# The rows of B in a Mamba scan: TensorE's selecting products and ScalarE's copies, or SBUF-to-SBUF DMAs

## The chip, the cores and the metric

The kernel runs on one core of one Trainium2 chip. The metric is device time in microseconds: the median of three runs is 295.14 us (293.34 to 295.16). The profile is one such execution; its span is 295.0 us.

## What is computed

A block of a model on x (4 batches of 256 tokens by 256 channels, float32) and a context of 4 x 256 x 128. A gated state-space layer runs on the context, and a quantised feed-forward layer behind it. Around the change stands the state-space layer:

```python
x = einsum('ed,bld->bel', in_proj_w, hidden_states)       # 256 channels, then a causal conv of 4 taps
u = silu(xc + conv_b[None, :, None])
x_dbl = einsum('ke,bel->bkl', x_proj_w, u)                # 8 + 16 + 16 rows of 256 tokens
dt_lo, Bm, Cm = x_dbl[:, :8], x_dbl[:, 8:24], x_dbl[:, 24:]
delta = softplus(einsum('er,brl->bel', dt_proj_w, dt_lo) + dt_proj_b[None, :, None])
A = -exp(A_log)                                           # 256 channels x 16 states
def step(state, xs):                                      # over the 256 tokens
    d_t, B_t, C_t, u_t = xs
    dA = exp(d_t[..., None] * A)
    state = state * dA + (d_t * u_t)[..., None] * B_t[:, None, :]
    y_t = einsum('ben,bn->be', state, C_t)
    return state, y_t
y = (y + D * u) * silu(z)
```

For each of the 16 states, row n of B (256 tokens, the same for all channels) multiplies delta * u of every channel. The channels lie on the 128 partitions (in two halves), so a row of B is needed on all 128 partitions.

## The kernel before

The work is cut into 32 steps: 4 batches of 8, each step with NB = 2 of the 16 states. The program is written out by hand for each engine, and each engine runs its list in order. Semaphores stand between the engines. A step m goes like this:

- **The rows of B.** `B_rows(m)` on TensorE: two products of a one-column selector (`sel`) with `bc3`, which holds B and C as three bf16 pieces, put the step's two rows on all 128 partitions in PSUM, in the half `PB` of the tensor `BC`. `copy_B(m)` on ScalarE copies them to `Bs[:, m % 4]` in SBUF. There is one `PB`, so product m waits for copy m - 1. `Bs` has RING = 4 places, so copy m waits until the drives of step m - 4 have read theirs.
- **The drives.** `drives(m)` on GpSimd multiplies du = delta * u by `Bs` (two instructions of 128x512). Steps 0 and 1 are done by VectorE (`first_drive`).
- **The decays.** `decays(m)` on ScalarE: four exponentials, behind the copy of the same step.
- **The scan** on VectorE, in its list in step order; it takes decay and drive, both kept in rings of four. GpSimd's drives m wait for scan m - 4.
- **The rows of C**, selected the same way by TensorE into `PC`, the product with them on VectorE (`times_C`), and TensorE's transposing sum of the products (`accumulate`).

B's rows, decays and drives are written AHEAD = 4 steps ahead of the scan. Between these steps stand, in the same lists, the front of batch k + 2 (projection, softplus), the norm and gate products of batch k - 1, and the quantised down projection of batch k - 2. What is left of batches 2 and 3 follows the last step. At the start, SP issues the loads of the inputs, four of them of 1 MB; afterwards SP has only the eight stores of the output (128 KB each), each after a wait for its result (L300 to L302). `high_pieces(n)` on ScalarE (L772) takes the first bf16 piece of batch n's B and C out of PSUM.

Of the kernel before, what the change touches and what calls it, by code (L numbers as in the profile page):

```python
# [12 lines left out]
P = 128  # L13
# [4 lines left out]
LC = L // P  # L18
# [36 lines left out]
def gated_ssm_ffn(nc, x, ctx_1024, g_xattn, g_ffn, in_proj_w, conv_w, conv_b, x_proj_w, dt_proj_w, dt_proj_b,  # L55
                  A_log, D, w_gate, w_up, w_down, ident, hadamard, out):
    stack = ExitStack()
    with stack:
        def sb(name, shape, dt=F32):
            return stack.enter_context(nc.sbuf_tensor(name, shape, dt))  # L60

        def sem(name):
            return stack.enter_context(nc.semaphore(name))
# [54 lines left out]
        diag = sb("diag", [P, HALF, P])  # L118

        Bs = sb("Bs", [P, RING, NB, L])  # L120
        decay = sb("decay", [P, RING, HALF, NB, L])
        drive = sb("drive", [P, RING, HALF, NB, L])
        state = sb("state", [P, STATES, HALF, NB, L])
# [64 lines left out]
        act_tap, dve_conv, dve_drive = sem("act_tap"), sem("dve_conv"), sem("dve_drive")  # L188
        had_built, dve_fold, pool_fold_last = sem("had_built"), sem("dve_fold"), sem("pool_fold_last")

        pe_B, act_B, act_decay, pool_drive, dve_scan, pe_C, dve_prod, pe_acc = (
            sem(n) for n in ("pe_B", "act_B", "act_decay", "pool_drive", "dve_scan", "pe_C", "dve_prod", "pe_acc"))

        pe_xin, dve_inwk, act_conv, act_u, pe_xdbl, dve_split, act_dtlo, pe_draw = (
            sem(n) for n in ("pe_xin", "dve_inwk", "act_conv", "act_u", "pe_xdbl", "dve_split", "act_dtlo", "pe_draw"))
# [9 lines left out]
            sem(n) for n in ("pool_fold", "pe_tp", "act_tp", "pe_h", "dve_sc", "act_tq", "dve_q2", "pe_q2T", "dve_q2T",  # L205
                             "pe_dn", "dve_out"))
        stored = [sem(f"stored_{t}") for t in range(LC)]

        pool_front_link = Chain(sem("pool_front_link"), 4)
        dve_front_link = Chain(sem("dve_front_link"), 3)  # L210
# [68 lines left out]
        @block.sync  # L279
        def _(sp):  # L280
            cr = tiles(ctx_1024)
            sp.dma_start(ctxs[:, 0], cr[:, 0:LC]).then_inc(ld_ctx0, 16)
            sp.dma_start(inw[:], in_proj_w.rearrange("(h p) d -> p h d", p=P)).then_inc(ld_inw, 16)
            sp.dma_start(xpw[:], x_proj_w).then_inc(ld_small, 16)
            sp.wait_ge(zeroed, 1)
            sp.dma_start(dtw[:, :, DT0:DT0 + DR], dt_proj_w.rearrange("(h p) r -> p h r", p=P)).then_inc(ld_small, 16)
            with nc.allow_non_contiguous_dma(reason="one value per partition"):
                for dst, src in ((cb, conv_b), (dtb, dt_proj_b), (dskip, D)):
                    sp.dma_start(dst[:], src.rearrange("(h p) -> p h", p=P)).then_inc(ld_conv, 16)
            sp.dma_start(ctxs[:, 1:B].rearrange("p b c d -> p (b c) d"), cr[:, LC:B * LC]).then_inc(ld_ctx, 16)  # L290
            sp.dma_start(wnat[:, 0].rearrange("p (a h) -> p a h", a=NI),
                         w_gate.rearrange("(a p) h -> p a h", p=P)).then_inc(ld_w[0], 16)
            sp.dma_start(xs[:].rearrange("p b c d -> p (b c) d"), tiles(x)).then_inc(ld_x, 16)
            sp.dma_start(wnat[:, 1].rearrange("p (a h) -> p a h", a=NI),
                         w_up.rearrange("(a p) h -> p a h", p=P)).then_inc(ld_w[1], 16)
            sp.dma_start(wnat[:, 2].rearrange("p (o i) -> p o i", o=HALF),
                         w_down.rearrange("(o p) i -> p o i", p=P)).then_inc(ld_w[2], 16)
            sp.dma_start(had[:], hadamard).then_inc(ld_had, 16)
            for b in range(B):
                for t in range(LC):  # L300
                    sp.wait_ge(dve_out, LC * b + t + 1)
                    sp.dma_start(tiles(out)[:, LC * b + t], ot[:, t]).then_inc(stored[t], 16)  # L302
            for t in range(LC):
                sp.wait_ge(stored[t], 16 * B)

# [2 lines left out]
        def _(pe):  # L308
# [36 lines left out]
            def setup_late():  # L345
# [4 lines left out]
                        at = (b - 1) * L + P * c  # L350
                        last = nc.tensor.transpose((PC if at < 512 else PY)[:, at % 512:at % 512 + P], ctxs[:, b, c], id32[:])
                last.then_inc(pe_setup, 1)

            def B_rows(m):

                b, j = divmod(m, STEPS)
                pe.wait_ge(dve_split, b + 1)
                pe.wait_ge(act_high0, b + 1)
                if m >= 1:
                    pe.wait_ge(act_B, m)  # L360
                else:
                    pe.wait_ge(act_setup, 2)
                for n in range(NB):
                    last = nc.tensor.matmul(PB[:, L * n:L * (n + 1)], row_pick(NB * j + n), bc3[:, b, :],  # L364
                                            start=True, stop=True)
                last.then_inc(pe_B, 1)

            def C_rows(m):
                b, j = divmod(m, STEPS)
# [11 lines left out]
            def row_pick(r):  # L381
                return sel[:, r:r + 1].to_broadcast([3 * 2 * DS, P])
# [140 lines left out]
            def hadamard_mm(f, t):  # L523

                pe.wait_ge(act_tp, LC * f + t + 1)
                if f == t == 0:
                    pe.wait_ge(had_built, 1)
                if (f, t) == (B - 2, 1):
                    pe.wait_ge(act_B, B * STEPS)
                    pe.wait_ge(dve_prod, B * STEPS)  # L530
                elif (f, t) == (B - 1, 0):
                    pe.wait_ge(act_tq, LC * f)
                elif f == B - 1:
                    pe.wait_ge(dve_mul, LC * f + 2)
                elif t == 0:
                    pe.wait_ge(dve_mul, LC * f + 2)
                else:
                    pe.wait_ge(act_tq, LC * f + 1)
                dst = transform_bank(f, t)
                for a in range(NI):  # L540
                    if f < B - 1:
                        last = nc.tensor.matmul(dst[:, E * (a // 2):E * (a // 2 + 1)], hT[:, t, a, :],  # L542
                                                had2[:, a % 2].rearrange("p i c -> p (i c)"),
                                                start=(a % 2 == 0), stop=(a % 2 == 1))
                    else:
                        last = nc.tensor.matmul(dst[:, P * a:P * (a + 1)], hT[:, t, a, :], had2[:, 0, 0],  # L546
                                                start=True, stop=True)
                last.then_inc(pe_h, 1)
# [53 lines left out]
            pe.wait_ge(dve_consts, 1)  # L602
            x_dbl(0)
            dt_proj(0)
            B_rows(0)
            setup_late()
            B_rows(1)
            in_proj(1, [0])
            B_rows(2)
            in_proj(1, [1])  # L610
            C_rows(0)
            for m in range(3, AHEAD):
                B_rows(m)
            for k in range(B):
                p, f, n = k - 2, k - 1, k + 2
                old, new, front = p >= 0, f >= 0, n < B
                for s in range(STEPS):
# [17 lines left out]
                    if s == 7:  # L635
                        if k == 0:
                            weight_T(5)
                    if g + AHEAD < B * STEPS:
                        B_rows(g + AHEAD)
                    if s == 1:  # L640
                        if k == 0:
                            x_dbl(1)
# [74 lines left out]
        def _(act):  # L717
# [4 lines left out]
                act.dma_start(gates[:, 1:2], g_ffn.partition_broadcast(P)).then_inc(ld_gate, 16)  # L722
                act.dma_start(alog[:], A_log.rearrange("(h p) n -> p h n", p=P)).then_inc(ld_gate, 16)

            def copy_B(m):
                act.wait_ge(pe_B, m + 1)
                if RING <= m < RING + DVE_DRIVES:
                    act.wait_ge(dve_drive, m - RING + 1)
                elif m >= RING:
                    act.wait_ge(pool_drive, drives_before(m - RING + 1))  # L730
                nc.scalar.copy(Bs[:, m % RING], PB.rearrange("p (n l) -> p n l", n=NB)).then_inc(act_B, 1)  # L731

            def decays(m):

                b, j = divmod(m, STEPS)
# [36 lines left out]
            def high_pieces(n):  # L772

                act.wait_ge(pe_xdbl, n + 1)
                if n >= 1:
                    act.wait_ge(dve_split, n)
                nc.scalar.copy(high[:], front_bank(n)[0:2 * 2 * DS, 0:L]).then_inc(act_high, 1)
                nc.scalar.copy(bc3[4 * DS:6 * DS, n], front_bank(n)[4 * DS:6 * DS, 0:L]).then_inc(act_high0, 1)
# [97 lines left out]
            act.wait_ge(pe_setup, 5)  # L876
            nc.scalar.copy(inwT[:].rearrange("p k e -> p (k e)"), UP[:]).then_inc(act_setup, 1)
            softplus(0)
            copy_B(0)
            act.wait_ge(pe_setup, 6)  # L880
            nc.scalar.copy(ctxT[:, 1:3], PC.rearrange("p (b l) -> p b l", b=2))
            nc.scalar.copy(ctxT[:, 3], PY[:, 0:L]).then_inc(act_setup, 1)
# [5 lines left out]
            act.wait_ge(decay_zeroed, 1)  # L888
            decays(0)
            for m in range(1, AHEAD):  # L890
                copy_B(m)
                decays(m)
            for k in range(B):
                p, f, n = k - 2, k - 1, k + 2
                old, new, front = p >= 0, f >= 0, n < B
                for s in range(STEPS):
# [19 lines left out]
                        if front:  # L916
                            high_pieces(n)
                    if g + AHEAD < B * STEPS:
                        copy_B(g + AHEAD)
                        decays(g + AHEAD)  # L920
                    if s == 0:
                        if k == 0:
# [52 lines left out]
        def _(pool):  # L975
            def drives(m):

                b, j = divmod(m, STEPS)
                pool.wait_ge(act_B, m + 1)
                pool.wait_ge(du_ready, b + 1)  # L980
                if m >= RING:
                    pool.wait_ge(dve_scan, m - RING + 1)
                for h in range(HALF):
                    last = nc.gpsimd.tensor_tensor(  # L984
                        drive[:, m % RING, h], du[:, b % 2, h, :].unsqueeze(1).to_broadcast([P, NB, L]),
                        Bs[:, m % RING], ALU.mult)
                last.then_inc(pool_drive, 1)
# [104 lines left out]
        def _(dve):  # L1092
# [48 lines left out]

            def first_drive(m):

                dve.wait_ge(act_B, m + 1)
                dve.wait_ge(du_ready, 1)
                for h in range(HALF):
                    last = nc.vector.tensor_tensor(drive[:, m, h], du[:, 0, h, :].unsqueeze(1).to_broadcast([P, NB, L]),
                                                   Bs[:, m], ALU.mult)
                last.then_inc(dve_drive, 1)
# [281 lines left out]
def tiles(t):  # L1431

    return t.rearrange("b l n -> (b l) n").rearrange("(c p) n -> p c n", p=P)
# [30 lines left out]
```

## Time and profile before

| | |
|---|---|
| median of 3 runs | 295.14 us (293.34 to 295.16) |
| span of the profiled execution | 295.0 us |
| VectorE busy | 255.7 us, 87% |
| GpSimd busy | 191.1 us, 65% |
| TensorE busy | 180.2 us, 61% |
| ScalarE busy | 163.9 us, 56% |
| first scan starts, last scan starts | 26.5 us, 241.2 us |
| bytes moved by DMA | 6.29 MB, nearly all in the first 22 us |

PE is TensorE's matmuls, PEld its weight loads, DVE VectorE, ACT ScalarE, POOL GpSimd, SPq the sequencer that issues DMAs. A name such as L984 is line 984 of the kernel before. Idle time is given with what ended it ("releaser"). Steps of the loop are not even: other work of VectorE lies between the scans.

### The profile page before, as it was taken

What the parts mean: (1) busy time and instruction counts of PE and PEld (TensorE: products, weight loads), DVE (VectorE), ACT (ScalarE), POOL (GpSimd) and SP (SyncE); (2) the same over time, 40 slices, a digit from 0 to 9 for tenths busy, and PEclk for the clock granted to TensorE, in tenths of its full rate; (3) what the DMA queues carried; (4) which work ended last, traced back from release to release, by engine and by line L of the source; (5) the groups of instructions that cost most, each with busy time, mean ns of one, the idle gap of its engine ahead of it and who ended that gap; (6) DMA issues with size and microseconds to landing.
All of it is one profiled execution on the core that took longest, in us unless ns stands there. A gap on an engine that the chain in (4) does not pass through costs nothing. (4 is left out here: it accounts for less than half of the span.)

```text
span 295.0 us, 3093 instructions
## 1 busy us (share of the span) xinstructions
PE 180.2 (61%) x988; PEld 140.0 (47%) x988; DVE 255.7 (87%) x295; ACT 163.9 (56%) x286; POOL 191.1 (65%) x137
## 2 busy tenths in 40 slices
PE   4567146661576456885665755868057397777583
PEld 2435045551464345564554644557046265563472
DVE  4399999989989999698899999986999997748974
ACT  1587948814772883698176656765075640544131
POOL 1000945798991399999997999499975608503800
PEclk9999659597768555978595976979669879979599
DMA  2990000000000000000000000000000000000001
GB/s 54 312 317 3 1 0 2 0 0 0 0 3 0 0 0 0 3 0 0 1 0 2 0 0 18 2 18 1 0 0 2 0 18 19 2 0 0 18 20 36
DMA packets 8145, 6.29 MB, mean 21 GB/s; under 512 B 2202, under 2 KB 7874, under 8 KB 8130
## 3 DMA queue, kind: packets, MB, share of 16 engines
q1 hardware_dynamic: 7154, 6.02, 6.3%
q10 hardware_dynamic: 976, 0.09, 0.2%
q8 instruction: 8, 0.13, 0.2%
q14 instruction: 7, 0.06, 0.1%
HBM read 5.05 MB, written 1.05 MB: 21 GB/s over the span
## 5 line engine op out<-in xcount | busy, mean ns | idle before, releaser
L984 POOL TENSOR_TENSOR drive<-du,Bs 128x512 f32<-128x512 f32 x60 | 104.8, 1771 | 48.1 <-ACT Bs L731 46.7
L1114 DVE TENSOR_TENSOR_SCAN state<-decay,drive 128x1024 f32<-128x1024 f32 x32 | 86.5, 2703 | 10.4 <-issue 7.4
L741 ACT ACTIVATE decay<-delta,zero_c,aneg 128x255 f32<-128x255 f32 x128 | 66.3, 592 | 8.9 <-DVE delta L1138 8.9
L393 PE MATMUL PY<-id,prod 128*128 128x128 f32 x256 | 46.0, 339 | 1.4 <-DVE prod L1156 1.4
L393 PEld LDWEIGHTS PY<-id,prod 128*128 128x128 f32 x256 | 40.9, 181 | 2.8 <-DVE prod L1156 1.6
L377 PE MATMUL BC<-bc,sel 96*128 96x256 bf16 x64 | 15.5, 333 | 42.9 <-DVE prod L1156 42.9
L1156 DVE TENSOR_TENSOR prod<-state,BC 128x1024 f32<-128x1024 f32 x32 | 38.5, 1204 | 0.6 <-PE BC L377 0.5
L377 PEld LDWEIGHTS BC<-bc,sel 96*128 96x128 bf16 x64 | 5.8, 108 | 51.6 <-issue 49.3
L836 ACT COPY hT<-GP 128x1024 f32<-128x1024 f32 x8 | 8.1, 1010 | 32.6 <-PE GP L520 32.6
L1009 POOL TENSOR_TENSOR wnat<-wnat 128x512 f32<-128x512 f32 x12 | 15.7, 1312 | 12.7 <-DVE wnat L1221 12.5
L1010 POOL TENSOR_TENSOR wnat<-wnat 128x512 f32<-128x512 f32 x12 | 23.6, 1967 | 0.0
L731 ACT COPY Bs<-BC 128x512 f32<-128x512 f32 x32 | 18.4, 575 | 9.1 <-PE BC L364 9.0
L364 PE MATMUL BC<-bc,sel 96*128 96x256 bf16 x64 | 15.1, 324 | 8.3 <-ACT Bs L731 8.1
L542 PE MATMUL UP<-wnat,hT 128*128 128x256 f32 x80 | 18.4, 382 | 1.1 <-ACT hT L836 1.1
L542 PEld LDWEIGHTS UP<-wnat,hT 128*128 128x128 f32 x80 | 14.8, 190 | 3.2 <-ACT hT L836 1.3
L504 PE MATMUL GP<-wT,qT 128*128 128x512 bf16 x32 | 9.9, 440 | 9.6 <-DVE ot L1249 7.0
L273 POOL TENSOR_TENSOR wnat<-wnat 128x160 f32<-128x160 f32 x6 | 4.1, 684 | 16.4 <-DVE wnat L1221 16.1
L520 PE MATMUL GP<-id,wnat 128*128 128x128 f32 x64 | 11.4, 338 | 4.7 <-POOL wnat L274 3.2
L842 ACT ACTIVATE ctxs<-UP,magic_c,sc 128x1024 f32<-128x1024 f32 x6 | 7.2, 1199 | 11.5 <-DVE sc L1231 11.5
L520 PEld LDWEIGHTS GP<-id,wnat 128*128 128x128 f32 x64 | 9.9, 181 | 6.0 <-DVE wnat L274 3.5
L596 PE MATMUL UP<-id,wq 128*128 128x128 bf16 x48 | 5.3, 276 | 12.3 <-DVE wq L1266 8.2
L364 PEld LDWEIGHTS BC<-bc,sel 96*128 96x128 bf16 x64 | 6.0, 112 | 13.7 <-issue 11.7
(182 smaller groups left out, 404.9 us busy)
## 6 DMA issues: line engine op xcount, KB each, us to landing
wnat<-in_L_ffn_w_gate_dram SPq DMA_DIRECT2D x1, 1024.0 KB, 9.7
xs<-in_x_dram SPq DMA_DIRECT2D x1, 1024.0 KB, 12.1
wnat<-in_L_ffn_w_up_dram SPq DMA_DIRECT2D x1, 1024.0 KB, 12.1
wnat<-in_L_ffn_w_down_dram SPq DMA_DIRECT2D x1, 1024.0 KB, 11.3
out_dram<-ot SPq DMA_DIRECT2D x8, 128.0 KB, 1.7
ctxs<-in_ctx_dram SPq DMA_DIRECT2D x1, 384.0 KB, 7.2
ctxs<-in_ctx_dram SPq DMA_DIRECT2D x1, 128.0 KB, 2.6
inw<-n_L_xattn_in_proj_w_dram SPq DMA_DIRECT2D x1, 128.0 KB, 2.6
```

The lines of the kernel that those rows point to most:

```text
L364: last = nc.tensor.matmul(PB[:, L * n:L * (n + 1)], row_pick(NB * j + n), bc3[:, b, :], start=True, stop=True)
L377: last = nc.tensor.matmul(PC[:, L * n:L * (n + 1)], row_pick(DS + NB * j + n), bc3[:, b, :], start=True, stop=True)
L393: last = nc.tensor.matmul(PY[:, E * c + P * h:E * c + P * (h + 1)], prod[:, g % RING, h, n, P * c:P * (c + 1)], id32[:], is_transpose=True ...
L520: last = nc.tensor.transpose(GP[:, P * a:P * (a + 1)], src[:, t, P * a:P * (a + 1)], id32[:])
L542: last = nc.tensor.matmul(dst[:, E * (a // 2):E * (a // 2 + 1)], hT[:, t, a, :], had2[:, a % 2].rearrange("p i c -> p (i c)"), start=(a % ...
L731: nc.scalar.copy(Bs[:, m % RING], PB.rearrange("p (n l) -> p n l", n=NB)).then_inc(act_B, 1)
L741: last = nc.scalar.activation(decay[:, m % RING, h, n, 1:L], delta[:, b % 2, h, 1:L], ACT.Exp, bias=zero_c[:], scale=aneg[:, h, NB * j + n ...
L984: last = nc.gpsimd.tensor_tensor(drive[:, m % RING, h], du[:, b % 2, h, :].unsqueeze(1).to_broadcast([P, NB, L]), Bs[:, m % RING], ALU.mult)
L1009: nc.gpsimd.tensor_tensor(dst[:, :, 0, :], src[:, :, 0, :], src[:, :, 1, :], ALU.add)
L1010: nc.gpsimd.tensor_tensor(dst[:, :, 1, :], src[:, :, 0, :], src[:, :, 1, :], ALU.subtract).then_inc(done, 1)
L1114: nc.vector.tensor_tensor_scan(state[:, g % STATES].rearrange("p h n l -> p (h n l)"), decay[:, g % RING].rearrange("p h n l -> p (h n l)" ...
L1156: nc.vector.tensor_tensor(prod[:, g % RING].rearrange("p h n l -> p h (n l)"), state[:, g % STATES].rearrange("p h n l -> p h (n l)"), PC. ...
```

## The change

TensorE's 64 products for B and ScalarE's 32 copies of 128x512 go. ScalarE copies the 16 rows of B of a batch once, from PSUM into a new small SBUF tensor `brow` (16 partitions x 256 tokens, for two batches), ahead of the first bf16 piece. SP then issues two DMAs for each step. Each reads one row of `brow`, 1,024 bytes on one partition, 128 times over, and writes it to the 128 partitions of `Bs`. Each place of the ring has its own semaphore, and the drives wait for it. The DMA of step m waits for the drives of step m - 4, as the copy did. SP's stores of batch 0 are placed between these DMAs (behind those of steps 26 and 29); the others follow the last of them.

```diff
+        brow = sb("brow", [DS, 2, L])
...
+        act_brow = sem("act_brow")
+        ld_B = [sem(f"ld_B{r}") for r in range(RING)]
...
-            for b in range(B):
+            def B_rows(m):
+                b, j = divmod(m, STEPS)
+                sp.wait_ge(act_brow, b + 1)
+                if RING <= m < RING + DVE_DRIVES:
+                    sp.wait_ge(dve_drive, m - RING + 1)
+                elif m >= RING:
+                    sp.wait_ge(pool_drive, drives_before(m - RING + 1))
+                for n in range(NB):
+                    row = brow[NB * j + n:NB * j + n + 1, b % 2]
+                    sp.dma_start(Bs[:, m % RING, n], row.unsqueeze(1).to_broadcast([1, P, L])).then_inc(ld_B[m % RING], 16)
...
+            for m in range(B * STEPS):
+                B_rows(m)
+                b, j = divmod(m - AHEAD - 2, STEPS)
+                if b >= 2 and j == 4:
+                    store(b - 2, 0)
+                if b >= 2 and j == 7:
+                    store(b - 2, 1)
+            for b in range(1, B):
                 for t in range(LC):
-                    sp.wait_ge(dve_out, LC * b + t + 1)
-                    sp.dma_start(tiles(out)[:, LC * b + t], ot[:, t]).then_inc(stored[t], 16)
+                    store(b, t)
...
-                for n in range(NB):
-                    last = nc.tensor.matmul(PB[:, L * n:L * (n + 1)], row_pick(NB * j + n), bc3[:, b, :],
-                                            start=True, stop=True)
-                last.then_inc(pe_B, 1)
...
-                nc.scalar.copy(Bs[:, m % RING], PB.rearrange("p (n l) -> p n l", n=NB)).then_inc(act_B, 1)
...
             def high_pieces(n):
 
                 act.wait_ge(pe_xdbl, n + 1)
+                if n >= 2:
+                    for r in range(RING):
+                        act.wait_ge(ld_B[r], 16 * NB * (n - 1) * STEPS // RING)
+                nc.scalar.copy(brow[:, n % 2], front_bank(n)[0:DS, 0:L]).then_inc(act_brow, 1)
...
             def drives(m):
-                pool.wait_ge(act_B, m + 1)
+                pool.wait_ge(ld_B[m % RING], 16 * NB * (m // RING + 1))
...
             def first_drive(m):
-                dve.wait_ge(act_B, m + 1)
+                dve.wait_ge(ld_B[m % RING], 16 * NB * (m // RING + 1))
```

On SP, the end of its list is the place. Before, behind the loads (had is the Hadamard matrix, the last of them; wnat the three weight matrices):

```order
L294 DMA wnat<-in_L_ffn_w_up_dram 128x8x256
L296 DMA wnat<-in_L_ffn_w_down_dram 128x2x1024
L298 DMA had<-in_hadamard_dram 128x128
L302 DMA out_dram<-ot 128x256 x8
L58 UNCONDITIONAL_BRANCH
```

And with the change:

```order
L297 DMA wnat<-in_L_ffn_w_up_dram 128x8x256
L299 DMA wnat<-in_L_ffn_w_down_dram 128x2x1024
L301 DMA had<-in_hadamard_dram 128x128
L313 DMA Bs<-brow 128x1x256 x54
L317 DMA out_dram<-ot 128x256
L313 DMA Bs<-brow 128x1x256 x6
L317 DMA out_dram<-ot 128x256
L313 DMA Bs<-brow 128x1x256 x4
L317 DMA out_dram<-ot 128x256 x6
```

64 DMAs have come in behind the loads, on the same queue, and two stores now stand between them. On ScalarE, the place is the end of the set-up and the first steps (dtlo: the low-rank rows of delta; high, bc: the bf16 pieces; inwT, ctxT: transposed projection weights and context). Before:

```order
L782 COPY dtlo<-GP 8x256
L777 CAST high<-GP 64x256
L778 CAST bc<-GP 32x256
L877 COPY inwT<-UP 128x1024
...
L797 ACTIVATE spl<-spe,one_c 128x512
L731 COPY Bs<-BC 128x512
L881 COPY ctxT<-BC 128x512
L882 COPY ctxT<-PY 128x256
...
L741 ACTIVATE decay<-delta,zero_c,aneg 128x255 x4
L731 COPY Bs<-BC 128x512
L741 ACTIVATE decay<-delta,zero_c,aneg 128x255 x4
```

And with the change:

```order
L781 COPY dtlo<-GP 8x256
L773 COPY brow<-GP 16x256
L776 CAST high<-GP 64x256
L777 CAST bc<-GP 32x256
L876 COPY inwT<-UP 128x1024
...
L796 ACTIVATE spl<-spe,one_c 128x512
L879 COPY ctxT<-BC 128x512
L880 COPY ctxT<-PY 128x256
...
L736 ACTIVATE decay<-delta,zero_c,aneg 128x255 x20
```

One copy of 16x256 has come in ahead of the bf16 pieces, the copies of B have gone, and the decays of steps 0 to 4 now follow each other with nothing between them.

## Rows read from the trace of the kernel before

**Rows 1.** The page's busy times: microseconds, share of the span, instructions.
```profile
PE 180.2 (61%) x988; PEld 140.0 (47%) x988; DVE 255.7 (87%) x295; ACT 163.9 (56%) x286; POOL 191.1 (65%) x137
```

**Rows 2.** Busy time of each engine (instructions) while the scans run.
```profile
core 0: us, PE busy (x) PEld busy (x) DVE busy (x) ACT busy (x) POOL busy (x), PEclk, DMA share, GB/s
26.50:241.00 214.50, 128.00 (x710) 101.78 (x711) 199.51 (x180) 131.89 (x238) 170.38 (x101) 0.75 0.01 3
```

**Rows 3.** Groups of instructions: shapes xcount, busy us, mean ns, idle before.
```profile
L984 POOL TENSOR_TENSOR drive<-du,Bs 128x512 f32<-128x512 f32 x60 | 104.8, 1771 | 48.1 <-ACT Bs L731 46.7
L1114 DVE TENSOR_TENSOR_SCAN state<-decay,drive 128x1024 f32<-128x1024 f32 x32 | 86.5, 2703 | 10.4 <-issue 7.4
L731 ACT COPY Bs<-BC 128x512 f32<-128x512 f32 x32 | 18.4, 575 | 9.1 <-PE BC L364 9.0
L364 PE MATMUL BC<-bc,sel 96*128 96x256 bf16 x64 | 15.1, 324 | 8.3 <-ACT Bs L731 8.1
```

**Rows 4.** VectorE's waits: what ended them, us in total, times, longest.
```profile
DVE state L1114 <- issue: 7.4, 5, 2.6
DVE state L1114 <- POOL drive L984: 2.8, 1, 2.8
```

**Rows 5.** Timeline of the start: start us, us, engine, line, operation, xcount.
```profile
15.85 0.37 ACT L777 CAST high<-GP 64x256 bf16<-64x256 f32 x1
24.30 0.69 DVE L248 TENSOR_TENSOR du<-delta,u 128x512 f32<-128x512 f32 x1
25.10 1.29 DVE L1147 TENSOR_TENSOR drive<-du,Bs 128x512 f32<-128x512 f32 x2
28.70 1.27 DVE L1147 TENSOR_TENSOR drive<-du,Bs 128x512 f32<-128x512 f32 x2
42.73 2.28 DVE L1114 TENSOR_TENSOR_SCAN state<-decay,drive 128x1024 f32<-128x1024 f32 x1
46.05 2.28 DVE L1114 TENSOR_TENSOR_SCAN state<-decay,drive 128x1024 f32<-128x1024 f32 x1
```

**Rows 6.** Stretches at the loads' end; last columns: DMA share, GB/s.
```profile
19.00:19.50 0.50, 0.50 (x5) 0.46 (x3) 0.50 (x3) 0.50 (x2) 0.00 (x0) 1.00 1.06 412
21.00:21.50 0.50, 0.00 (x0) 0.00 (x0) 0.47 (x8) 0.50 (x3) 0.00 (x0) 1.00 0.34 120
22.00:23.00 1.00, 0.92 (x4) 0.57 (x3) 0.93 (x3) 0.80 (x4) 0.00 (x0) 1.00 0.07 25
23.00:24.00 1.00, 1.00 (x4) 0.82 (x3) 0.97 (x2) 0.00 (x0) 0.00 (x0) 1.00 0.00 0
```

**Rows 7.** DMA in the window 179.5:183.5, in 40 slices of 0.1 us.
```profile
GB/s 0 0 0 0 0 0 0 0 0 0 0 0 143 338 328 348 144 10 0 0 0 0 0 0 0 0 0 0 0 0 0 0 0 0 0 0 0 0 0 0
DMA packets 144, 0.13 MB, mean 33 GB/s; under 512 B 16, under 2 KB 144, under 8 KB 144
out_dram<-ot SPq DMA_DIRECT2D x1, 128.0 KB, 1.7
```

**Rows 8.** Timeline of SPq: two small issues among the first.
```profile
3.69 0.47 SPq L289 DMA_DIRECT2D dskip<-in_L_xattn_D_dram  x1
4.21 0.47 SPq L290 DMA_DIRECT2D ctxs<-in_ctx_dram  x1
```

**Rows 9.** Timeline around the last scans and the program's end.
```profile
212.69 2.48 POOL L984 TENSOR_TENSOR drive<-du,Bs 128x512 f32<-128x512 f32 x2
241.16 2.28 DVE L1114 TENSOR_TENSOR_SCAN state<-decay,drive 128x1024 f32<-128x1024 f32 x1
292.30 0.48 DVE L1249 SCALAR_TENSOR_TENSOR ot<-X,dq,x 128x256 f32<-128x256 f32 x1 [0.48 <-PE X L572]
```

More of the change, by code:

```diff
@@ L189, in gated_ssm_ffn @@
         had_built, dve_fold, pool_fold_last = sem("had_built"), sem("dve_fold"), sem("pool_fold_last")
-        pe_B, act_B, act_decay, pool_drive, dve_scan, pe_C, dve_prod, pe_acc = (
-            sem(n) for n in ("pe_B", "act_B", "act_decay", "pool_drive", "dve_scan", "pe_C", "dve_prod", "pe_acc"))
+        act_decay, pool_drive, dve_scan, pe_C, dve_prod, pe_acc = (
+            sem(n) for n in ("act_decay", "pool_drive", "dve_scan", "pe_C", "dve_prod", "pe_acc"))
         pe_xin, dve_inwk, act_conv, act_u, pe_xdbl, dve_split, act_dtlo, pe_draw = (
@@ L298, in _, with store @@
             sp.dma_start(had[:], hadamard).then_inc(ld_had, 16)
-            for b in range(B):
+            def B_rows(m):
[8 more added lines that the diff above has]
+                    sp.dma_start(Bs[:, m % RING, n], row.unsqueeze(1).to_broadcast([1, P, L])).then_inc(ld_B[m % RING], 16)
+            def store(b, t):
+                sp.wait_ge(dve_out, LC * b + t + 1)
+                sp.dma_start(tiles(out)[:, LC * b + t], ot[:, t]).then_inc(stored[t], 16)
+            for m in range(B * STEPS):
[6 more added lines that the diff above has]
+            for b in range(1, B):
                 for t in range(LC):
-                    sp.wait_ge(dve_out, LC * b + t + 1)
-                    sp.dma_start(tiles(out)[:, LC * b + t], ot[:, t]).then_inc(stored[t], 16)
+                    store(b, t)
             for t in range(LC):
@@ L352, in setup_late @@
                 last.then_inc(pe_setup, 1)
[L354 to L362, printed above, removed]
-                for n in range(NB):
-                    last = nc.tensor.matmul(PB[:, L * n:L * (n + 1)], row_pick(NB * j + n), bc3[:, b, :],
-                                            start=True, stop=True)
-                last.then_inc(pe_B, 1)
             def C_rows(m):
@@ L528, in hadamard_mm @@
                 if (f, t) == (B - 2, 1):
-                    pe.wait_ge(act_B, B * STEPS)
                     pe.wait_ge(dve_prod, B * STEPS)
@@ L604, in _ @@
             dt_proj(0)
-            B_rows(0)
             setup_late()
[L607 to L610, printed above, removed]
+            in_proj(1)
             C_rows(0)
-            for m in range(3, AHEAD):
-                B_rows(m)
             for k in range(B):
@@ L637, in _ @@
                             weight_T(5)
-                    if g + AHEAD < B * STEPS:
-                        B_rows(g + AHEAD)
                     if s == 1:
@@ L723, in setup_loads @@
                 act.dma_start(alog[:], A_log.rearrange("(h p) n -> p h n", p=P)).then_inc(ld_gate, 16)
[L725 to L730, printed above, removed]
-                nc.scalar.copy(Bs[:, m % RING], PB.rearrange("p (n l) -> p n l", n=NB)).then_inc(act_B, 1)
             def decays(m):
@@ L878, in _ @@
             softplus(0)
-            copy_B(0)
             act.wait_ge(pe_setup, 6)
@@ L890, in _ @@
             for m in range(1, AHEAD):
-                copy_B(m)
                 decays(m)
@@ L918, in _ @@
                     if g + AHEAD < B * STEPS:
-                        copy_B(g + AHEAD)
                         decays(g + AHEAD)
```

## The prediction

> **What bounds the kernel now.** I read the busy times first, then the stretch in which the scans run, then the waits of the two engines that the rows of B feed, and last the DMAs. In the busy times [rows 1] the reader sees one engine far ahead: VectorE at 87%. In the stretch of the scans [rows 2] it is 199.5 us busy of 214.5, which is 93%, while ScalarE has 61% and TensorE 60%. So what is taken from ScalarE and TensorE there can bring at most what VectorE waits for them. The 16 DMA engines are all but idle in this stretch (share 0.01). GpSimd waits long for the copies of B: 46.7 us in all [rows 3]. But VectorE waits for GpSimd's drives only once, 2.8 us, and sits idle before scans for 7.4 us in five other places, where the trace names no releaser [rows 4]. Idle time of GpSimd ahead of a ring of four that is full costs nothing.
>
> **What is removed.** 64 products of 324 ns (15.1 us) on TensorE and 32 copies of 575 ns (18.4 us) on ScalarE [rows 3]. Both are off the path: the work that hides them is VectorE's own 199.5 us. At the most the change gives back VectorE's waits before scans, 2.8 + 7.4 = 10.2 us [rows 4], if all of them are drives or decays that come late; at the least nothing. GpSimd's drives, started earlier, meet other instructions of VectorE; scans last 2,703 ns in the mean, and 2.28 us in the row at 42.73 us [rows 3, 5], so some 0.4 us of each moves with such meetings and may fall either way. I take half of the waits, 5 us.
>
> **What is added on ScalarE.** Four copies of 16x256, each priced like the cast of 64x256 in 0.37 us [rows 5]: 1.5 us, under VectorE's work. The first delays the bf16 pieces by 0.4 us, where VectorE has other work up to du at 24.30 us. I price it at nothing; its cover gone, it costs 0.4 us. The new wait in it, for all rows of batch n - 2, stands behind decays(10) or decays(18), and the next decays and the pieces are queued behind it. It ends once the rows of step 7 (or 15) have landed, which scan 7 (or 15) needs in any case. The decays are by then three steps ahead, so it is hidden as long as rows arrive at a steady pace.
>
> **What is added on SP.** 64 issues of about 0.47 us [rows 8], 0.94 us a step of 6.7 us: free. Each issue pair waits for the drives of step m - 4; three other steps lie between, so a landing that takes some us is hidden. Behind the waits stand the stores of batch 0. They are due at steps 26 and 29, after results that VectorE has by then, and the later stores have the same results to wait for as before.
>
> **What a pair of DMAs costs.** This is the term that decides. The trace has no DMA out of one partition, so I bound it from both sides. A step moves 2 x 128 x 1,024 = 262,144 bytes. *Lower end:* a store of 128 KB, in which every engine reads partitions of its own, keeps the DMA engines at work for some 0.5 us and lands 1.7 us after its issue [rows 7]. At that rate a pair takes about 1 us of the engines and lands within 1.7 + 0.5 + 0.5 = 2.7 us of the first issue. *Upper end:* in every transfer of the trace the sixteen engines work on sixteen different groups of partitions. The best rate is 412 GB/s [rows 6], which is 25.8 GB/s for each engine and its partitions. Here all sixteen engines read the same partition, both rows of a step lie side by side, and no row shows one place of SBUF giving more than 25.8 GB/s. If it gives just that, the pair takes 262,144 / 25,750 = 10.2 us. I take the upper end, because only the reads are gathered in one place, and the rate of one place is the only rate that the rows have for it; the store reads from all. From it I take off 0.2 us for the overlap where the rows move on to other partitions: 10.0 us a step.
>
> The Trainium skill has this rule: "SBUF — State Buffer", section "Door 1: The DMA port swizzle", maps partitions 0 to 3 to one port, and so on in fours, and gives a port 27.2 GB/s (27.6 measured for partitions 0..3). By it the pair costs 9.6 us, and the sum below would be 386 us. No row of this trace has such a transfer.
>
> **The sum.** The pace of the scans is 214.5 / 32 = 6.7 us a step [rows 2] (31 distances and a bit, so this errs to the low side by 3%). 10.0 us is more, so the transfers set the end. The queue is never empty: when the rows of step m land, its drives take 2.5 us [rows 9] and the two issues 0.9 us, and meanwhile those of m + 1 to m + 3 are 30 us of work. The rows begin once the loads ahead of them on the same queue are through: 120 GB/s at 21 us, 25 at 22, none from 23 on [rows 6]; I take 21.5 us. `brow` is ready at about 16.3 us [rows 5], in time.
> - Rows of step 31 landed: 21.5 + 32 x 10.0 + 1.0 (issue to landing less the time of moving, from 1.7 and 0.5) = 342.5 us.
> - Drives of step 31: 2.5 us [rows 9], so its scan starts at 345.0 us.
> - From the last scan's start to the end: 295.0 - 241.2 = 53.8 us [rows 9]. All of it is VectorE's list and what follows it, and stays.
> - Together 398.8 us, against a span of 295.0. The span stands 0.1 us below the median of the runs, so 399 us. VectorE then waits before nearly every scan, and its other work is hidden in these waits. What is late next is nothing: every engine has more than 3 us a step to spare.
>
> The change is therefore slower by about 104 us, or 35%.
>
> **The rivals.**
> 1. *The transfers are hidden.* Each engine gets its own rate from the one partition, a pair lands in 2.7 us, and VectorE stays the bound. For it speaks that nothing in the trace shows a limit on reading; and 128 reads of the same kilobyte may well cost less than 128 different ones. Against it: that sixteen readers of one place would then draw over 300 GB/s from it, twelve times what the rows show of a place. Price: nothing; the first rows land at about 21.5 + 2.7 = 24.2 us, before the drives at 25.10 us [rows 5]. Gain 5 us of 10.2: 290 us, between 285 and 298. This is the other side; it decides from a pair below about 4 us, and for the mean step from 6.7 us down. Chance 0.24. The Trainium skill's "DMA: Bandwidth & Descriptors", section "Where 436 GB/s comes from", gives copies between SBUF and SBUF the whole fabric, 435 GB/s; by that alone a pair would take 0.6 us, and this rival would be right.
> 2. *Two groups of partitions at a time.* With four steps in the ring, fast engines may run on to later rows in other partitions while slow ones finish: 5.1 us a pair, below 6.7 us. Then only the start is late. Rows of step 0 land at 22.5 + 5.1 = 27.6 us and those of step 1 at 32.7 us, against drives at 25.10 and 28.70 us [rows 5]: 4.0 us. The scans of steps 2 and 3, 3.3 us apart before [rows 5], add 1 to 2 us. 295.1 + 5.5 = 301 us, up to 330 where the overlap is half. Chance 0.09.
> 3. *One partition gives less than its group.* If it gives half of 25.8 GB/s, a pair costs 20.4 us: 22.5 + 652.8 + 2.5 + 53.8 = 732 us. Rows cannot rule it out, since in all of them an engine has several partitions before it. Chance 0.06.
> 4. *A transfer runs on fewer engines than sixteen*, or each packet costs its engine alone. On one engine at 25.8 GB/s the price is again 10.2 us a pair, so it goes with the forecast and could be told from it only by the DMA share: one sixteenth instead of nearly all.
>
> **How the numbers follow.** The forecast has 0.61. Its own range is 370 to 440 us: 9.1 to 11.3 us a pair, with the start 1 us either way. A measurement of this kernel tells about 1% from no change. Faster by more than 1% (under 292.2) comes from rival 1 alone, 0.13. Within 1%: rival 1 again, 0.08. Slower: the forecast, rivals 2 and 3, and 0.03 of rival 1, where GpSimd's earlier drives fall on VectorE's two-input instructions: 0.79. The range has to hold both sides: from 287 us, which leaves out 0.04 of rival 1, to 440 us, which leaves out rival 3 and 0.04 of the forecast: 0.14 outside.
>
> **What would show it.** In the profile of the changed kernel: a DMA share near 1 from 22 us to 340 us at about 25 GB/s; DMAs of `Bs` that take 10 us and more from issue to landing; VectorE's waits before scans of about 100 us in all, released by GpSimd's drives, and these by DMAs; scans 10 us apart. Right mechanism and wrong size would show as an even distance of scans other than 10 us. The prediction is wrong if a DMA of `Bs` lands in 2 to 3 us and the share stays in the tenths: then rival 1 holds, and GpSimd's 46.7 us of waits are gone without VectorE's time changing much. Bursts of two overlapping pairs would show rival 2.

## The result and the profile after

The changed kernel takes 351.61 us (median of 4 runs, 350.41 to 353.57) against 295.15 us before in the same comparison. The ratio is 1.19, with a 95% interval of 1.183 to 1.198. The span of the profiled execution is 348.4 us. The ratios compare executions in the chip's faster state; of the four of the first experiment below one was not, at 378.57 us.

The page of the changed kernel, against [rows 1] and [rows 3]:

```profile
PE 184.5 (53%) x918; PEld 144.4 (41%) x924; DVE 232.4 (67%) x295; ACT 149.6 (43%) x258; POOL 168.1 (48%) x137
L980 POOL TENSOR_TENSOR drive<-du,Bs 128x512 f32<-128x512 f32 x60 | 81.6, 1381 | 134.2 <-DMA Bs<-brow 129.8
L1110 DVE TENSOR_TENSOR_SCAN state<-decay,drive 128x1024 f32<-128x1024 f32 x32 | 82.3, 2573 | 65.3 <-issue 51.0
Bs<-brow SPq DMA_DIRECT2D x64, 128.0 KB, 15.4
```

VectorE has fallen from 87% to 67%: it waits 65.3 us before scans, where it waited 10.4. GpSimd waits 129.8 us for the rows of B. Most of VectorE's waits carry "issue", with no releaser, so on VectorE alone the cause is not to be seen; it stands one engine further back, on GpSimd. A DMA of `Bs` lands 15.4 us after its issue (median), most of it spent behind others in the queue (the steps below are 8.43 us apart, so one of the two DMAs takes about 4.2 us of its own). VectorE has the same 295 instructions and is busy 23 us less with them than before; why was not followed. The stretch in which the rows are moved, in the columns of [rows 2]:

```profile
23.00:292.00 269.00, 136.76 (x672) 108.96 (x675) 180.26 (x185) 122.39 (x216) 144.87 (x99) 0.68 0.79 32
```

The DMA engines are at 0.79 of their time for 32 GB/s. At the loads' end they moved 412 GB/s [rows 6]. Closer, the same in 40 slices of the window 150:200 (1.25 us each):

```profile
GB/s 27 33 65 64 28 26 26 27 26 26 26 34 26 26 27 58 48 26 26 26 26 25 26 26 26 26 26 26 64 60 58 26 26 26 26 26 26 26 26 26
```

The rate stands at 26 GB/s and doubles to about 60 for a few slices, three times in 50 us. GpSimd's drives show what goes with it:

```profile
181.26 2.49 POOL L980 TENSOR_TENSOR drive<-du,Bs 128x512 f32<-128x512 f32 x2 [0.55 <-DMA Bs<-brow]
188.41 2.50 POOL L980 TENSOR_TENSOR drive<-du,Bs 128x512 f32<-128x512 f32 x2 [4.65 <-DMA Bs<-brow]
...
197.54 2.50 POOL L980 TENSOR_TENSOR drive<-du,Bs 128x512 f32<-128x512 f32 x2 [2.21 <-DMA Bs<-brow]
204.50 2.50 POOL L980 TENSOR_TENSOR drive<-du,Bs 128x512 f32<-128x512 f32 x2 [4.46 <-DMA Bs<-brow]
```

Steps come 7.2, 9.1 and 7.0 us apart in turn. A step takes two partitions of `brow`, so after every second step the rows move on to the next four. The last drives and the last scan, the rows that answer to [rows 9]:

```profile
292.77 2.48 POOL L980 TENSOR_TENSOR drive<-du,Bs 128x512 f32<-128x512 f32 x2 [6.85 <-DMA Bs<-brow]
...
295.34 2.29 DVE L1110 TENSOR_TENSOR_SCAN state<-decay,drive 128x1024 f32<-128x1024 f32 x1 [5.33 <-issue]
```

From the drives of step 2 (GpSimd's first, at 48.33 us) to those of step 31 there are 29 steps in 244.4 us: 8.43 us a step, or 31 GB/s.

### The profile page after: what moved, and what is told of

It is laid out like the page before. It is cut to its first block and busy times, and to the rows that moved or that the text cites. A ratio compares the mean times of both kernels' runs of the same rounds, so it can differ in the third digit from the quotient of the medians.

```text
span 348.4 us, 2962 instructions
## 1 busy us (share of the span) xinstructions
PE 184.5 (53%) x918; PEld 144.4 (41%) x924; DVE 232.4 (67%) x295; ACT 149.6 (43%) x258; POOL 168.1 (48%) x137
## 5 line engine op out<-in xcount | busy, mean ns | idle before, releaser
L980 POOL TENSOR_TENSOR drive<-du,Bs 128x512 f32<-128x512 f32 x60 | 81.6, 1381 | 134.2 <-DMA Bs<-brow 129.8
L1110 DVE TENSOR_TENSOR_SCAN state<-decay,drive 128x1024 f32<-128x1024 f32 x32 | 82.3, 2573 | 65.3 <-issue 51.0
L736 ACT ACTIVATE decay<-delta,zero_c,aneg 128x255 f32<-128x255 f32 x128 | 65.5, 587 | 20.7 <-DVE delta L1134 10.7
L389 PE MATMUL BC<-bc,sel 96*128 96x256 bf16 x64 | 16.3, 349 | 70.7 <-DVE prod L1152 70.5
L405 PE MATMUL PY<-id,prod 128*128 128x128 f32 x256 | 50.7, 364 | 0.3 <-DVE prod L1152 0.3
L405 PEld LDWEIGHTS PY<-id,prod 128*128 128x128 f32 x256 | 45.1, 195 | 2.1 <-DVE prod L1152 0.7
L1152 DVE TENSOR_TENSOR prod<-state,BC 128x1024 f32<-128x1024 f32 x32 | 38.6, 1207 | 10.8 <-PE BC L389 10.7
L389 PEld LDWEIGHTS BC<-bc,sel 96*128 96x128 bf16 x64 | 5.5, 110 | 80.1 <-issue 79.2
L1006 POOL TENSOR_TENSOR wnat<-wnat 128x512 f32<-128x512 f32 x12 | 27.6, 2298 | 0.0
L553 PE MATMUL UP<-wnat,hT 128*128 128x256 f32 x80 | 21.3, 426 | 1.1 <-ACT hT L835 1.1
L1005 POOL TENSOR_TENSOR wnat<-wnat 128x512 f32<-128x512 f32 x12 | 15.7, 1310 | 3.8 <-DVE wnat L1217 3.6
L765 ACT ACTIVATE sz<-zn,zero_c 128x512 f32<-128x512 f32 x4 | 2.9, 717 | 29.5 <-POOL zn L992 29.5
L992 POOL TENSOR_SCALAR zn<-xs,r,mr 128x256 f32<-128x256 f32 x8 | 10.5, 1317 | 0.0
## 6 DMA issues: line engine op xcount, KB each, us to landing
Bs<-brow SPq DMA_DIRECT2D x64, 128.0 KB, 15.4
```

Source lines behind the costliest of these rows:

```text
L389: last = nc.tensor.matmul(PC[:, L * n:L * (n + 1)], row_pick(DS + NB * j + n), bc3[:, b, :], start=True, stop=True)
L405: last = nc.tensor.matmul(PY[:, E * c + P * h:E * c + P * (h + 1)], prod[:, g % RING, h, n, P * c:P * (c + 1)], id32[:], is_transpose=True ...
L736: last = nc.scalar.activation(decay[:, m % RING, h, n, 1:L], delta[:, b % 2, h, 1:L], ACT.Exp, bias=zero_c[:], scale=aneg[:, h, NB * j + n ...
L980: last = nc.gpsimd.tensor_tensor(drive[:, m % RING, h], du[:, b % 2, h, :].unsqueeze(1).to_broadcast([P, NB, L]), Bs[:, m % RING], ALU.mult)
L992: last = nc.gpsimd.tensor_scalar(zn[:, h], xs[:, n, h], r1[:, i:i + 1], mr1[:, i:i + 1], ALU.mult, ALU.add)
L1005: nc.gpsimd.tensor_tensor(dst[:, :, 0, :], src[:, :, 0, :], src[:, :, 1, :], ALU.add)
```

## The experiments

The theory to be tested (A): the place that is read sets the rate, a group of neighbouring partitions gives about 26 GB/s whoever reads, and where the rows move on, two groups give at once. Its rivals: (B) the cost is one of the DMAs, whatever they read; (C) a single partition is the limit, not its group. The ratios are to the kernel before, run on the same chip.

### Each engine reads its own partitions

```diff
-                    row = brow[NB * j + n:NB * j + n + 1, b % 2]
-                    sp.dma_start(Bs[:, m % RING, n], row.unsqueeze(1).to_broadcast([1, P, L])).then_inc(...)
+                    sp.dma_start(Bs[:, m % RING, n], brow[:, b % 2]).then_inc(...)      # brow on 128 partitions
```

> The same 64 DMAs of 128 packets of 1,024 bytes, at the same places with the same waits, but each reads brow on all 128 partitions, one row per partition, instead of one row 128 times (the values of B are then not those of the reference: brow is filled with a constant on partitions 16 to 127). Theory A, the place that is read sets the rate: each engine reads its own partitions, a pair lands in about 2.7 us, the transfers are hidden, 285 to 298 us, which is the rival 1 of the prediction and shows what the whole rest of the change is worth. Theory B, the cost is one of the DMAs themselves (their packets of 1 KB, SBUF to SBUF, or SP's issue), whatever they read: 8.4 us a step as before, 350 us.

Measured: 293.23 us, ratio 0.988 (0.980 to 0.996). The page's row for the DMAs, VectorE's and GpSimd's waits (us in total, times, longest), and the group of the scans:

```profile
Bs<-brow SPq DMA_DIRECT2D x64, 128.0 KB, 2.1
DVE state L1110 <- issue: 6.5, 4, 2.6
POOL drive L979 <- DMA Bs<-brow: 15.8, 1, 15.8
L1110 DVE TENSOR_TENSOR_SCAN state<-decay,drive 128x1024 f32<-128x1024 f32 x32 | 84.1, 2627 | 7.6 <-issue 6.5 <-ACT decay L735 0.9
```

The number of DMAs, their packets, bytes, places and waits are those of the changed kernel, and it is 58 us faster. Theory B falls. What is left of GpSimd's waits for rows is one, at the start. It also prices the rest of the change: with the transfers hidden, VectorE's waits before scans go from 10.4 us [rows 3] to 7.6, its busy time from 255.7 to 253.4, and the kernel is about 1% faster.

### All rows from partition 0, and from partitions 0 to 3

```diff
-                    row = brow[NB * j + n:NB * j + n + 1, b % 2]
+                    row = brow[0:1, b % 2]                     # the first kernel
+                    r = (NB * j + n) % 4                       # the second
+                    row = brow[r:r + 1, b % 2]
```

> All rows are read from partition 0 of brow (so every step gets row 0 of B); nothing else is changed. The changed kernel's steps came 8.4 us apart, alternately about 7 and 10, where its rows move to the next four partitions every second step. Theory A, a group of four partitions gives about 26 to 27 GB/s and the moves let two groups work at once: with no moves 9.6 to 10.2 us a step, evenly spaced, 388 to 410 us. Theory B, the place doesn't matter: 350 us with the same alternation. Theory C, one partition gives less than its group of four: clearly above 410 us here and less in the next kernel.

> The rows are read from partitions 0 to 3 in turn (so the steps get rows 0 to 3 of B again and again); nothing else is changed. Theory A: as with partition 0 alone, 388 to 410 us, steps evenly spaced. Theory C, the single partition is the limit: faster than with partition 0 alone. Theory B: 350 us.

Measured: 395.49 us (ratio 1.333, 1.322 to 1.344) and 396.22 us (1.335, 1.324 to 1.346), two executions each. GpSimd's drives in the first:

```profile
150.10 2.48 POOL L980 TENSOR_TENSOR drive<-du,Bs 128x512 f32<-128x512 f32 x2 [7.44 <-DMA Bs<-brow]
160.03 2.49 POOL L980 TENSOR_TENSOR drive<-du,Bs 128x512 f32<-128x512 f32 x2 [7.44 <-DMA Bs<-brow]
...
169.96 2.49 POOL L980 TENSOR_TENSOR drive<-du,Bs 128x512 f32<-128x512 f32 x2 [0.27 <-DMA Bs<-brow]
...
179.89 2.49 POOL L980 TENSOR_TENSOR drive<-du,Bs 128x512 f32<-128x512 f32 x2 [3.08 <-DMA Bs<-brow]
```

and in the second:

```profile
160.02 2.49 POOL L981 TENSOR_TENSOR drive<-du,Bs 128x512 f32<-128x512 f32 x2 [7.50 <-DMA Bs<-brow]
...
179.88 2.49 POOL L981 TENSOR_TENSOR drive<-du,Bs 128x512 f32<-128x512 f32 x2 [3.14 <-DMA Bs<-brow]
```

The steps are 9.93 us apart, evenly: 262,144 bytes in 9.93 us is 26.4 GB/s. One partition gives as much as four neighbours in turn, so theory C falls, and rival 3 of the prediction with it. The alternation of 7 and 9 to 10 us is gone with the moves: they are what made 8.43 us out of 9.93.

### Rows from sixteen groups, and from two

```diff
+                    r = 4 * j + 64 * n                         # sixteen groups; brow is [P, 2, L]
+                    row = brow[r:r + 1, b % 2]
```

> The two rows of a step are read from partitions 4j and 64 + 4j, so that no two of 16 DMAs in a row read the same group of partitions (brow is filled with a constant where no row of B lies, so the values of B are not those of the reference). Theory A in its strict form, all engines go through the DMAs together and one row always comes from one place: 9.6 to 10.2 us a step or the 8.4 of now, 350 us or more. Theory A with engines that drift apart over the DMAs in the queue: two or more places give at once, the pair falls below 6.7 us, and the time is near 295 to 305 us. Theory B: 350 us.

Measured: 295.76 us, ratio 0.997 (0.993 to 1.001). For two groups:

```diff
-                nc.scalar.copy(brow[:, n % 2], front_bank(n)[0:DS, 0:L]).then_inc(act_brow, 1)
+                nc.scalar.copy(brow[0:DS, n % 2], front_bank(n)[0:DS, 0:L])
+                nc.scalar.copy(brow[4 * DS:5 * DS, n % 2], front_bank(n)[4 * DS:5 * DS, 0:L]).then_inc(act_brow, 1)
...
-                    row = brow[NB * j + n:NB * j + n + 1, b % 2]
+                    r = 4 * DS * n + NB * j + n
+                    row = brow[r:r + 1, b % 2]
```

> ScalarE also copies the third set of B's rows, which the projection leaves on partitions 64 to 79, and the second row of each step is read from there, so the two rows of a step lie in groups of partitions far apart. Nothing else is changed. Theory A with engines that drift over the DMAs in the queue, as the run with sixteen groups showed: two places at a time, about 5 us a step, 295 to 303 us (the start is late). Theory A with engines in step: no gain over the changed kernel, 350 us, since within one DMA there is still one place. A place is not a group of four but all of the lower partitions: the same as theory A here, but the run with sixteen groups would then have been no faster than this one.

Measured: 298.41 us, ratio 1.011 (1.003 to 1.020). The stretch 25:45, in which the first rows are behind and the queue is full: the changed kernel, then sixteen groups, then two (the last number is GB/s).

```profile
25.00:45.00 20.00, 3.58 (x12) 2.59 (x11) 10.36 (x13) 11.68 (x23) 0.00 (x0) 0.65 0.79 31
```

```profile
25.00:45.00 20.00, 6.60 (x26) 4.86 (x24) 18.39 (x17) 11.61 (x23) 10.08 (x6) 0.67 0.78 56
```

```profile
25.00:45.00 20.00, 7.15 (x27) 5.29 (x25) 16.98 (x16) 11.84 (x23) 6.84 (x4) 0.67 0.76 56
```

Both give 56 GB/s, twice the rate of one place, and a pair then costs 4.7 us, which VectorE's pace covers. One DMA still reads one place, so the doubling has to come from engines that are already at a later DMA than others. The semaphore records in the traces show it: they have sixteen landings for each DMA, 32 for a step. In the changed kernel, up to step 25, the first landing of a step comes 0.8 to 2.0 us before the last one of the step before where the rows move to other partitions, and between 0.7 us after it and 0.3 us before it where they stay. With two groups it comes 1.7 to 2.8 us before it (steps 2 to 7).

The run with two groups reads the two rows of a step from different halves of the partitions, which leaves a rival: a place could be all of the lower partitions, and not a group of four. Then sixteen groups would have given no more than two, as they did. It falls by the changed kernel itself: all its rows lie in partitions 0 to 15, and its rate doubles where they move from one four to the next, while the reads of partitions 0 to 3 alone never sped up.

Engines at different DMAs were rival 2 of the prediction. It put the cost at the start: in the run with two groups the second pair of VectorE's drives begins at 30.71 us against 28.70 [rows 5], but the last scan at 241.5 against 241.2 [rows 9], so nearly all of that was made up. Where the 1.1% of its median comes from is not shown. That sixteen groups give no more than two was not expected. It fits that the engines lie only a little apart: there just one to three of the 32 landings of a step come before the last one of the step before, by 0.3 to 0.9 us (steps 2 to 8). What holds the engines that close together is not shown.

### One row of the two

```diff
-                for n in range(NB):
-                    row = brow[NB * j + n:NB * j + n + 1, b % 2]
-                    sp.dma_start(Bs[:, m % RING, n], ...)
+                row = brow[NB * j + 1:NB * j + 2, b % 2]
+                sp.dma_start(Bs[:, m % RING, 1], ...)
+                nc.scalar.copy(Bs[:, m % RING, 0], PB[:, 0:L]).then_inc(act_B, 1)   # and TensorE's product for it
```

> Of each step's two rows the first is spread by TensorE and ScalarE as in the kernel before (half the product, half the copy), the second by one DMA as in the changed kernel. Half the load on the place that is read: 9.9 us for two rows of one group (measured from partition 0 alone) gives 4.2 to 5.0 us a step, below the 6.7 us at which VectorE goes. Theory A, one place gives 26.4 GB/s and only that made the change slow: hidden, 290 to 298 us. If a fixed cost of each DMA beside the work (SP, the queue, GpSimd's waits) made it slow, about half of the loss stays: 320 us or so.

Measured: 299.03 us, ratio 1.014 (1.005 to 1.024). With half the load the loss is 1.4% instead of 19%, not half of it: the transfers cost next to nothing until they are slower than VectorE's pace, as theory A has it. The median is 1 us above what was expected. VectorE waited 5.3 us for the rows of C in the early steps, which the kernel before did not (0.6 us in all). The mixture of the two paths is not the reason: the same wait is 4.6 us with sixteen groups, 5.8 with two and 5.8 with half rows (below), and the two runs whose transfers are fastest, from each engine's own partitions and from DRAM, have none that TensorE ended. It goes with first rows that come late; the changed kernel's own, of 10.7 us, is taken apart in the next section.

### The rows from DRAM

```diff
+                act.wait_ge(act_brow, n + 1)
+                act.dma_start(bdram[n], brow[:, n % 2]).then_inc(st_brow[n], 16)
...
-                sp.wait_ge(act_brow, b + 1)
+                sp.wait_ge(st_brow[b], 16)
-                    sp.dma_start(Bs[:, m % RING, n], row.unsqueeze(1).to_broadcast([1, P, L])).then_inc(...)
+                    sp.dma_start(Bs[:, m % RING, n], bdram[b, NB * j + n].partition_broadcast(P)).then_inc(...)
```

> brow is first stored to DRAM (one DMA of 16 KB per batch, issued by ScalarE), and each row is read 128 times from there instead of from one partition. Theory A, and DRAM gives one kilobyte to sixteen engines at their full rate: a pair lands in about 3 us, hidden, 289 to 296 us, as with reads from each engine's own partitions; the first rows come 1 to 3 us later than there. If reads of one kilobyte are slow wherever it lies: more than 6.7 us a pair and 310 us or more.

Measured: 296.02 us, ratio 1.001 (0.997 to 1.005): the same as the kernel before. The DMAs, and the rate in the window 24:44 (0.5 us a slice):

```profile
Bs<-bdram SPq DMA_DIRECT2D x64, 128.0 KB, 3.0
GB/s 252 219 242 219 279 232 109 2 72 148 162 133 27 0 0 16 0 0 0 0 0 14 100 178 242 250 273 250 219 47 0 0 0 0 0 0 0 0 0 0
```

128 reads of one kilobyte in DRAM go at up to 279 GB/s, ten times what one place in SBUF gives. It is the detour through memory that takes the limit away. The time is within the noise of no change, and not better: VectorE is the bound again, with 253.1 us busy and the same 7.6 us of waits before scans as with each engine's own partitions.

### Half the bytes in as many packets

```diff
-                    row = brow[NB * j + n:NB * j + n + 1, b % 2]
-                    sp.dma_start(Bs[:, m % RING, n], row.unsqueeze(1).to_broadcast([1, P, L])).then_inc(...)
+                    row = brow[0:1, b % 2, 0:L // 2]
+                    sp.dma_start(Bs[:, m % RING, n, 0:L // 2], row.unsqueeze(1).to_broadcast([1, P, L // 2])).then_inc(...)
```

> As the run that reads everything from partition 0, but each of the 128 packets of a DMA carries the first 512 bytes of the row instead of 1,024 (the other half of Bs keeps a constant, so the result is not the reference's). The number of DMAs and of packets is the same. If the place gives bytes at a rate (26.4 GB/s, measured there), a pair takes 5.0 us, below VectorE's 6.7, and the time is 293 to 303 us. If it gives packets at a rate (256 in 9.93 us, 39 ns each), nothing changes: 9.9 us a step and 395 us. In between, a fixed part per packet: for a pair over 6.7 us the steps show it directly, below that the landings do.

Measured: 297.81 us, ratio 1.007 (1.003 to 1.012). At the start the rows are still behind, and the drives show the price of a pair:

```profile
36.16 3.56 POOL L980 TENSOR_TENSOR drive<-du,Bs 128x512 f32<-128x512 f32 x2 [26.32 <-DMA Bs<-brow]
41.33 4.04 POOL L980 TENSOR_TENSOR drive<-du,Bs 128x512 f32<-128x512 f32 x2 [1.61 <-DMA Bs<-brow]
46.37 3.65 POOL L980 TENSOR_TENSOR drive<-du,Bs 128x512 f32<-128x512 f32 x2 [1.01 <-DMA Bs<-brow]
```

131,072 bytes in 5.1 us is 25.7 GB/s, against 26.4 with packets twice as long. The place gives bytes at a rate; a packet of half the size costs half, and 3% more. So of rival 4 of the prediction the packet's own cost falls, here and with theory B. Its other half, a transfer that runs on one engine, falls by the changed kernel's DMA share: 0.79, and not one sixteenth.

## Why the prediction was right in kind and too high in size

- **What bounds the kernel.** Right. With the transfers hidden, the whole rest of the change brought 1% at most by the medians (0.988, and 1.001 by way of DRAM), as VectorE's 93% in [rows 2] allowed; the 5 us of the prediction were 3.6 by the first of these and nothing by the second. GpSimd's 46.7 us of waits were worth nothing.
- **The rate of one place.** Right. The 25.8 GB/s that each engine had of its own partitions [rows 6] was the rate of a place with sixteen readers: 26.4 measured, 9.93 us a pair against the 10.2 of the upper end. The Trainium skill ("SBUF — State Buffer", section "Door 1: The DMA port swizzle") gives a port 27.2 GB/s, from which 9.6 us is an estimate; the trace agrees to 3%. That partitions 0 to 3 give no more than partition 0 alone agrees with its map, and so does the doubling once rows lie in other groups. Why sixteen groups give only twice one, the map does not say. The forecast's 25.8 GB/s was in part luck: the 412 GB/s behind it are loads that write into SBUF, and no row had a read of one place by sixteen engines.
- **The step that failed is the overlap at the moves.** The prediction took 0.2 us a step off for it, without a row to work from. It is 9.93 - 8.43 = 1.50 us a step, or 3.0 us for each move. For a few slices two places give at once, and the rate is 60 GB/s instead of 26. Put into the sum, 8.43 for 10.0 over 32 steps takes off 50.2 us: 398.8 - 50.2 = 348.6 us, against a span of 348.4. Of the 50.2 us, 8.6 are the rate (9.93 for 10.2, the term above) and 41.6 are the overlap (1.50 for 0.2). All else in the sum held to within 1 us: the start at 21.5 us, the drives of the last step, and the 53.8 us behind the last scan (53.0 measured, from 295.34 us). The range of the forecast alone, 370 to 440 us, missed the time for this term; the whole range, 287 to 440 us, has it only because it had to reach down to rival 1. The slowdown is 56 us, where 104 were forecast; rival 2 had named the mechanism, but as a state of its own and not as one that comes and goes with the moves.
- **The ring and SP.** Right in what they cost, and not in how. The last DMAs landed when the sum has them, so SP's 64 issues cost nothing, but one took SP 4.4 us in the median and not 0.47:

```profile
L313 SPq DMA_DIRECT2D Bs<-brow x64: 559/4430/7210, 16.3 to 274.8; - x64
```

  (nanoseconds: shortest, median, longest). With each engine's own partitions the median is 0.6 us, so an issue is held up when the DMAs ahead of it are slow. They land 15.4 us after their issue: less than two steps are queued, and not the 30 us of work of the prediction.
- **"What is late next is nothing."** Wrong in one place, without a price. GpSimd's normalising of z stands behind the drives of step 4, ScalarE's silu behind it, and on TensorE the rows of C behind the transposes of that:

```profile
64.78 2.48 POOL L980 TENSOR_TENSOR drive<-du,Bs 128x512 f32<-128x512 f32 x2 [7.04 <-DMA Bs<-brow]
67.25 1.09 POOL L992 TENSOR_SCALAR zn<-xs,r,mr 128x256 f32<-128x256 f32 x2
68.38 0.72 ACT L765 ACTIVATE sz<-zn,zero_c 128x512 f32<-128x512 f32 x1 [29.47 <-POOL zn L992]
...
70.80 1.22 DVE L1152 TENSOR_TENSOR prod<-state,BC 128x1024 f32<-128x1024 f32 x1 [10.68 <-PE BC L389]
```

  VectorE waited 10.7 us for the rows of C there. The transfers went on meanwhile, and since they set the end, this was no loss: the sum has no room for it.
- **What would show it.** The share was to be near 1 at 25 GB/s; it was 0.79 at 32. The waits before scans were to be about 100 us; they were 65.3, and 20 more before the products and the first drives. The steps were not at an even distance, but 7 and 9 to 10 us apart in turn, with bursts in the rate; that is the prediction's own sign for rival 2, here at the moves alone. The releaser that the trace would name was not GpSimd's drives but "issue", for 51.0 us of it.

No kernel of these beats the one before by more than the noise and computes the same. The one that read each engine's own partitions needs the rows spread already.

## What to carry to other kernels

Before a broadcast goes from an engine to the DMA queues, count the bytes that are read from one place, every repetition included, divide them by the rate of one place, and set that time against the pace of the step. 128 copies of a row are read from one partition at 26 GB/s although sixteen engines read, so 256 KB a step is 10 us and not 1. Where the source can lie in DRAM, or be turned over between groups of partitions, the same DMAs are hidden. And an engine's long waits (46.7 us here) are worth only what the bound engine waits for it.

## What the runs showed of the hardware

- One partition of SBUF, or four neighbours in turn, gives 26.4 GB/s to sixteen DMA engines. The rate counts bytes: 25.7 GB/s with packets of 512 bytes.
- With the rows of successive DMAs in two groups or in sixteen, it is 56 GB/s in either case. The engines are then at different DMAs of the queue at the same time, by the landings, but only a little apart; why not more is open.
- One kilobyte of DRAM was read 128 times at up to 279 GB/s, and 128 KB landed in 3.0 us; from each engine's own partitions in SBUF, 2.1 us.
- The DMA share does not tell the rate: 0.79 stood for 32 GB/s where one place was read, and 1.06 for 412 GB/s in the loads [rows 6].
